# One transpose of the score maxima per batch in place of two, placed inside the key projections, with three other moves in the schedule

## The chip, the cores and the metric

The kernel runs on one core of one Trainium2 chip. The metric is the device time of one execution in microseconds (us); for the kernel before it is the median of three runs. The core has five queues that run beside each other and meet only at semaphores: TensorE (PE: matmuls, with its weight loads shown as PEld), VectorE (DVE), ScalarE (ACT), GpSimd (POOL) and SyncE (SP, which issues DMAs here).

## The reference

x is (32, 112, 512), the context (32, 375, 512); all is float32. Per batch: a layer norm of x, queries from it, keys and values from the 257 image rows and 118 text rows of the context with separate weights, an RMS norm on queries and keys, two softmax attentions over 16 heads of 32, their sum, an output projection and a residual:

```
q = rms_norm(linear(x, q_w, q_b), norm_q_w)
k = rms_norm(linear(ctx_txt, k_w, k_b), norm_k_w);  v = linear(ctx_txt, v_w, v_b)
k_img, v_img = the same from ctx_img with their own weights
out = attention(q, k, v) + attention(q, k_img, v_img)
x = x + linear(out, o_w, o_b)
```

Then a second layer norm, a router score for each row, the 14 best rows of each batch (`top_k`), and for these 448 rows alone a block of causal attention over all of them and a gated MLP, whose result is written back into the rows.

## The kernel before

The code has one hand-written instruction stream for each engine; there is no planner. What an engine does next is the order in which its stream lists the helpers, and each helper begins with the semaphore waits that it needs (`wait_ge`).

After a first stage (queries of all batches, weights), `over_batches` runs one pass for each of the 32 batches: pass 0 and pass 1, a hardware loop for passes 2 to 29, pass 30, and a pass 31 (`last`). In `body(i, n, m, p, q)`, i is the batch whose attention is made, n = i + 1 the one whose keys are projected, m = i + 2 the one whose context is loaded, p = i - 1 the one that gets its output projection, and q = i - 2 the one that gets its router score and rank. The passes follow each other without a barrier. After them comes the block on the chosen rows.

Matmuls of projections are made of three fp32r products (high by high, high by low, low by high), so each context tile is split on chip. ScalarE rounds it (`split_ctx`, L780, `ctx_hi`), and GpSimd subtracts the rounded part (L547, `ctx_lo`), once for the 118 text columns (part 0) and once for the 256 image columns (part 1). The semaphore `ctx_lo_done` counts these subtractions. `keys(n, k)` projects tile k of the keys with 12 matmuls of 512 columns (L1535 to L1537); tile 0 is text, tiles 1 and 2 are image. In front of tile 0 and of tile 1 it waits for the subtraction of its part (L1585).

For each of the four groups of four heads, `scores` (L1625) makes row scores in PSUM banks 2 to 5, `group_max` (VectorE, L1151 and L1152) takes a maximum for each head over text and over image keys into `top`. `turn_top` (TensorE, L1636) transposes `top`, once for groups 0 and 1 and once for groups 2 and 3, and ScalarE copies each result to `topT` (L834). `scores_T(i, g)` makes the scores once more, transposed, with the maxima subtracted: a small product of a 0/-1 matrix with `topT` for the text rows (L1660) and one for the image rows (L1664), and products of keys and queries in float32 (L1654). ScalarE takes the exponentials (L843, L845), GpSimd adds the two image tiles (`sum_image`, L581), VectorE adds one row (`add_tail`, L1157), and `weighted_values` (L1691) makes the four sums that `normalise` (VectorE, L1163 to L1169) divides. `o_hi` (ScalarE, L863) and `o_rest` (VectorE, L1173) split the result for `output` (TensorE, bank 1). `residual` (GpSimd, L589) adds the output bias to the reloaded x rows, `add_residual` and `ln2` (VectorE) and `normalise_h` (GpSimd) follow, then `score` (VectorE, L1200) and on GpSimd `output` (L585), which stands in the queue between the two parts of `split_ctx`. `turn_score` (TensorE, L1641) spreads the score of each row over a row of PSUM bank 7 and `ranks` (VectorE, L1191, L1193) counts how many are larger.

The order on TensorE around the change:

```
scores(i, 2); values(i, 1); turn_top(i, 0); scores(i, 3); keys(n, 0)
turn_top(i, 1); scores_T(i, 0); keys(n, 1); turn_score(q)
scores_T(i, 1); keys(n, 2); scores_T(i, 2)
```

Of the kernel before, what the change touches and what calls it, by code (L numbers as in the profile page):

```python
# [56 lines left out]
def build(nc, t, out):  # L57
    with ExitStack() as ctx:
# [109 lines left out]
        top = [p1(f"top{e}", [L, P]) for e in range(2)]  # L168
        topT = [p1(f"topT{e}", [P, L], F32R) for e in range(2)]
# [199 lines left out]
        def prob_of(g):  # L369
            return prob_txt_keys[g % 3], prob_img_keys[g % 3]  # L370

# [171 lines left out]
        def _(pool):  # L543
# [47 lines left out]
            def pre():  # L591
# [7 lines left out]
                nc.gpsimd.memset(top[0][:], 0.0)  # L599
                nc.gpsimd.memset(top[1][:], 0.0)  # L600
# [48 lines left out]
            def body(i, n, m, p, q):  # L649
# [33 lines left out]
            def last(i, p, q):  # L683
# [91 lines left out]
        def _(act):  # L775
# [56 lines left out]
            def turn_top(i, e):  # L832
                act.wait_ge(top_full, 2 * i + e + 1)
                nc.scalar.activation(topT[e][:], ps[:, 6, e * L:(e + 1) * L], ACT.Copy).then_inc(topT_ready, 1)  # L834
# [82 lines left out]
            def body(i, n, m, p, q):  # L917
# [42 lines left out]
            def last(i, p, q):  # L960
# [5 lines left out]
                turn_top(i, 0)  # L966
                token_squares(0)
                value_image(i, 1)
                token_squares(1)
                turn_top(i, 1)  # L970
                exps(i, 0)
# [134 lines left out]
        def _(dve):  # L1106
# [39 lines left out]
            def group_max(i, g):  # L1146
                dve.wait_ge(s_full, 4 * i + g + 1)
                if g % 2 == 0:
                    dve.wait_ge(top_full, 2 * i - 1 + g // 2 if not isinstance(i, int) or i else 0)
                rows = top[g // 2][:].rearrange("l (j r) -> l j r", j=GH)  # L1150
# [9 lines left out]
            def normalise(i, g):  # L1160
                dve.wait_ge(pv_full, 4 * i + g + 1)
                bank = ps[:, 6 + g % 2, 0:4 * L].rearrange("p (k q) -> p k q", k=4)
                nc.vector.reciprocal(rec[:], bank[:, 2:4]).then_inc(norm_step, 1)  # L1163
# [5 lines left out]
                nc.vector.scalar_tensor_tensor(oT[:, g], o_two[:, 0], v_bias[:, g:g + 1], o_two[:, 1], ALU.add, ALU.add).then_inc(pv_done, 1)  # L1169

# [16 lines left out]
            def ranks(q):  # L1187

                dve.wait_ge(score_turned, q + 1)
                score_row = ps[0:L, 7, 2 * L:3 * L]  # L1190
# [96 lines left out]
            def body(i, n, m, p, q):  # L1287
# [34 lines left out]
                add_tail(i, 2)  # L1322
                tail_keys(n)
# [18 lines left out]
            def last(i, p, q):  # L1342
# [8 lines left out]
                ranks(q)  # L1351
# [23 lines left out]
            ranks(B - 2)  # L1375
# [11 lines left out]
            ranks(B - 1)  # L1387
# [144 lines left out]
        def _(pe):  # L1532
# [95 lines left out]
            def turn_top(i, e):  # L1628
                pe.wait_ge(s_done, 4 * i + 2 * e + 2)
                if e:  # L1630
                    pe.wait_ge(topT_ready, 2 * i + 1)
# [109 lines left out]
            def body(i, n, m, p, q):  # L1741
# [30 lines left out]
                if q is not None:  # L1772
                    pe.wait_ge(rank_done, q + 1)
# [301 lines left out]
```

## Time and profile before

| what | value |
|---|---|
| three runs | 1526.75, 1527.26, 1528.58 us |
| profiled execution, its own time | 1524.64 us |
| its span | 1522.9 us |
| TensorE matmul busy | 1497.2 us (98%) |
| VectorE, ScalarE, GpSimd busy | 1182.6, 715.8, 688.5 us (78%, 47%, 45%) |
| chain that ended last | PE 89%, DVE 5%, ACT 3% |
| granted TensorE clock | 0.999 of full speed |

"Busy" is the share of time in which at least one instruction of the engine is under way. The chain that ended last is followed back from the last instruction of the span, at each step to what released it, so its shares tell which engine set the time. The passes over the batches lie between about 120 and 1172 us of the span. In the timeline views a row is one instruction or several merged ones, and "x4" is their number; matmuls are pipelined, so the time that one costs is the distance from start to start, not its duration.

### The profile page before, as it was taken

The numbers are of one execution on the slowest core, as the hardware profiler recorded it, in microseconds if no ns is written. First come the engines' busy times: TensorE is split into PE (matmuls) and PEld (weight loads), VectorE is DVE, ScalarE is ACT, GpSimd is POOL, SyncE is SP. The second block draws the span as 40 slices with busy tenths as digits, with TensorE's granted clock in tenths as the row PEclk, the third lists the DMA queues.
The fourth block names the chain that finished last, engine by engine and source line by source line (L and its number), as shares of the span: only waits on it lengthen the run. The fifth ranks groups of instructions, "written<-read, shape, count | busy, mean of one in ns | idle before, by whom it ended". The sixth has DMA issues, their size and how long they took to land.

```text
span 1522.9 us, 41381 instructions
## 1 busy us (share of the span) xinstructions
PE 1497.2 (98%) x16220; PEld 1186.7 (78%) x16220; DVE 1182.6 (78%) x1884; ACT 715.8 (47%) x1458; POOL 688.5 (45%) x727
## 2 busy tenths in 40 slices
PE   8999999999999999999999999999999999999997
PEld 6777777777777777777777777777777787778997
DVE  6765788888888888888888888888887686554986
ACT  5874444444444444444444444444445124655431
POOL 3543344454444454444444444544445692114752
PEclk9999999999999999999999999999999999999999
DMA  8961121211111221112221112121125524010000
GB/s 262 346 207 60 39 63 52 77 56 50 56 54 59 67 66 50 56 50 62 62 70 50 56 50 62 58 75 50 56 87 154 196 111 167 28 56 29 1 1 25
DMA packets 70199, 121.04 MB, mean 79 GB/s; under 512 B 21840, under 2 KB 36528, under 8 KB 68608
## 3 DMA queue, kind: packets, MB, share of 16 engines
q1 hardware_dynamic: 69312, 117.54, 23.9%
q0 software_dynamic: 832, 2.75, 0.7%
q8 instruction: 36, 0.59, 0.2%
q14 instruction: 19, 0.16, 0.0%
HBM read 89.93 MB, written 30.34 MB: 79 GB/s over the span
## 4 chain that ended last, share of the span: by engine, by line
PE 89%; DVE 5%; ACT 3%; issue 1%; DMA 1%; POOL 1%; ACTq 0%; DVEq 0%; POOLq 0%
PE ps L1535 21%; PE ps L1536 19%; PE ps L1537 18%; PE ps L1691 10%; PE ps L1654 6%; PE ps L1625 3%; PE ps L1596 3%; PE ps L1660 2%; PE ps L1900 2%; PE ps L1917 2%; PE ps L1909 1%; PE ps L1664 1%; DMA q_dram<-q_turned 1%; DVE rec L1163 1%; PE ps L1636 0%
## 5 line engine op out<-in xcount | busy, mean ns | idle before, releaser
L547 POOL TENSOR_TENSOR ctx_lo<-ctx_raw,ctx_hi 128x472 fp32r<-128x472 f32 (+1 forms) x62 | 112.8, 1819 | 192.8 <-ACT ctx_hi L780 192.8
L1163 DVE RECIPROCAL rec<-ps 128x224 f32<-128x224 f32 x128 | 198.3, 1549 | 1.1 <-PE ps L1691 0.9
L581 POOL TENSOR_TENSOR prob_img<-prob 128x448 f32<-128x448 f32 x93 | 107.9, 1160 | 149.3 <-ACT prob L845 149.3
L1152 DVE TENSOR_REDUCE top<-ps 112x4 f32<-112x1028 f32 x128 | 156.2, 1220 | 0.0
L1151 DVE TENSOR_REDUCE top<-ps 112x4 f32<-112x472 f32 x128 | 83.1, 649 | 72.9 <-PE ps L1625 72.9
L1654 PE MATMUL ps<-q_all,k_all 32*128 32x112 f32 (+1 forms) x3072 | 125.2, 274 | 0.0
L1535 PE MATMUL ps<-w_v_img_hi,ctx_hi 128*128 128x512 f32 x256 | 107.4, 419 | 0.0
L1535 PE MATMUL ps<-w_k_img_hi,ctx_hi 128*128 128x512 f32 x256 | 107.1, 418 | 0.0
L843 ACT ACTIVATE prob<-ps 119x448 f32<-119x448 f32 x96 | 52.4, 546 | 114.8 <-PE ps L1654 114.8
L1654 PEld LDWEIGHTS ps<-q_all,k_all 32*128 32x128 f32 (+1 forms) x3072 | 105.4, 184 | 0.0
L1536 PE MATMUL ps<-w_k_img_lo,ctx_hi 128*128 128x512 f32 x256 | 101.1, 395 | 0.0
L1536 PE MATMUL ps<-w_v_img_lo,ctx_hi 128*128 128x512 f32 x256 | 101.0, 395 | 0.0
L1537 PE MATMUL ps<-w_k_img_hi,ctx_lo 128*128 128x512 f32 x256 | 100.8, 394 | 0.0
L1537 PE MATMUL ps<-w_v_img_hi,ctx_lo 128*128 128x512 f32 x256 | 100.7, 393 | 0.0
L845 ACT ACTIVATE prob<-ps 128x896 f32<-128x896 f32 x96 | 87.7, 913 | 0.0
L780 ACT ACTIVATE ctx_hi<-ctx_raw 128x472 fp32r<-128x472 f32 x64 | 52.9, 827 | 69.8 <-PE ps L1537 69.8
L1137 DVE SCALAR_TENSOR_TENSOR proj<-proj,rstd,w_img 128x512 f32<-128x512 f32 x64 | 48.0, 750 | 45.4 <-POOL rstd L574 45.4
L1537 PE MATMUL ps<-hT_hi,ring_lo 128*128 128x448 f32 x224 | 81.9, 366 | 0.0
L813 ACT ACTIVATE sq_junk<-proj 128x513 bf16<-128x513 f32 (+1 forms) x96 | 61.1, 636 | 34.8 <-DVE proj L1131 34.8
L574 POOL TENSOR_TENSOR rstd<-sq_sum,neg_half 128x1 f32<-128x1 f32 x96 | 64.8, 675 | 16.0 <-ACT sq_junk L813 16.0
L1173 DVE SCALAR_TENSOR_TENSOR oT_lo<-o_space,oT_hi 128x448 fp32r<-128x448 f32 x31 | 39.7, 1282 | 40.7 <-ACT oT_hi L863 40.7
L1157 DVE SCALAR_TENSOR_TENSOR prob_img<-prob,ones_last,prob_img 23x448 f32<-23x448 f32 x93 | 64.5, 693 | 6.1 <-POOL prob_img L581 3.1
(358 smaller groups left out, 4410.7 us busy)
## 6 DMA issues: line engine op xcount, KB each, us to landing
ctx_raw<-in_ctx_dram SPq DMA_DIRECT2D x32, 748.0 KB, 4.2
xh_dram<-xh SPq DMA_DIRECT2D x32, 448.0 KB
xc<-in_xT_dram SPq DMA_DIRECT2D x28, 256.0 KB, 4.5
q_dram<-q_turned SPq DMA_DIRECT2D x28, 256.0 KB, 4.6
q_all<-q_dram SPq DMA_DIRECT2D x32, 224.0 KB, 3.1
out_dram<-out_sb SPq DMA_DIRECT2D x32, 224.0 KB, 2.3
xh<-in_x_dram SPq DMA_DIRECT2D x31, 224.0 KB, 2.9
proj<-in_x_dram SPq DMA_DIRECT2D x21, 256.0 KB, 5.1
```

What stands on the lines that cost most here:

```text
L547: nc.gpsimd.tensor_tensor(ctx_lo[:, :, cols], ctx_raw[:, :, cols], ctx_hi[:, :, cols].bitcast(F32), ALU.subtract).then_inc(ctx_lo_done, 1)
L574: nc.gpsimd.tensor_tensor(rstd1[:, k:k + 1], sq_sum[:, k:k + 1], neg_half[:], ALU.pow).then_inc(rms_inv, 1)
L581: nc.gpsimd.tensor_tensor(prob_img[:, g % 2], image[:, 0, :], image[:, 1, :], ALU.add).then_inc(img_summed, 1)
L845: nc.scalar.activation(image.rearrange("p c (j q) -> p j c q", j=GH), ps[:, 2:6, L:3 * L].rearrange("p j (c q) -> p j c q", c=2), ACT.Exp) ...
L1151: nc.vector.tensor_reduce(rows[:, :, 2 * g], ps[0:L, 2:6, 0:TXT], AX.X, ALU.max)
L1152: nc.vector.tensor_reduce(rows[:, :, 2 * g + 1], ps[0:L, 2:6, TAIL:CTX], AX.X, ALU.max).then_inc(s_done, 1)
L1163: nc.vector.reciprocal(rec[:], bank[:, 2:4]).then_inc(norm_step, 1)
L1535: nc.tensor.matmul(o_, a_hi, b_hi, start=start, stop=False)
L1536: nc.tensor.matmul(o_, a_hi, b_lo, start=False, stop=False)
L1537: return nc.tensor.matmul(o_, a_lo, b_hi, start=False, stop=stop)
L1654: made = nc.tensor.matmul(ps[0:rows, 2 + j, c * L:(c + 1) * L], k_all[head, g, at:at + rows], q_all[head, g, :], start=False, stop=stop)
L1691: last = nc.tensor.matmul(ps[HD * j:HD * (j + 1), bank, slot * L:(slot + 1) * L], left[0:rows, cols], right[0:rows, L * j:L * (j + 1)], st ...
```

## The change

`top` and `topT` become one tile each, and `turn_top` runs once per pass, for all groups; ScalarE copies once. In the passes its place on TensorE is behind `keys(n, 0)`, and the first six of the twelve matmuls of `keys(n, 1)` are put between it and `scores_T(i, 0)`. The other six and the first three of `keys(n, 2)` come between `scores_T(i, 0)` and `scores_T(i, 1)`, and the last nine between `scores_T(i, 1)` and `scores_T(i, 2)`. Inside `scores_T` the two products with `topT` now come first, before the products of keys and queries. `turn_score` writes to bank 2 and stands in front of the transposes of the new keys; `ranks` moves on VectorE to behind `add_tail(i, 2)`, and TensorE waits for it at the end of the pass. On GpSimd `residual` comes before the first `sum_image`; on ScalarE `o_hi` comes before the first exponentials; on VectorE the bias of key tile 1 is added before `add_tail(i, 0)`. A filler tile keeps the addresses of the other tiles. The last pass gets the same in its own order.

```diff
@@ gpsimd, body
                 split_ctx(n, 1)
-                sum_image(i, 0)
-                inverse_rms(n, 1)
                 if p is None:
                     pool.wait_ge(out_rows_loaded, 16 * 2)
                 else:
                     residual(p)
+                sum_image(i, 0)
+                inverse_rms(n, 1)
                 sum_image(i, 1)
@@ gpsimd, last
                 output(q)
+                residual(p)
                 pool.wait_ge(oT_lo_done, i)
+                pool.wait_ge(topT_ready, i + 1)
                 value_weights_lo(0, 0)
+                normalise_h(p)
                 value_weights_lo(0, 1).then_inc(w_lo_done, 1)
-                residual(p)
-                normalise_h(p)
@@ scalar, body
-                turn_top(i, 0)
-                turn_top(i, 1)
-                exps(i, 0)
+                turn_top(i)
                 if p is not None:
                     o_hi(p)
+                exps(i, 0)
@@ vector, body
                     o_rest(p)
+                add_bias(n, 2)
                 add_tail(i, 0)
-                if q is not None:
-                    ranks(q)
                 scale_k(n, 1)
-                add_bias(n, 2)
...
                 add_tail(i, 2)
+                if q is not None:
+                    ranks(q, ps[0:L, 2, 0:L])
                 tail_keys(n)
@@ tensor, keys
-            def keys(n, k):
+            def keys(n, k, chunks=range(KC)):
...
-                if k < 2:
-                    pe.wait_ge(ctx_lo_done, 2 * n + k + 1)
-                if not isinstance(n, int) or n or k == 2:
-                    pe.wait_ge(done, slot)
-                project(bank[0:rows], ctx_hi, ctx_lo, cols, w).then_inc(full, 1)
+                if 0 in chunks:
+                    if k < 2:
+                        pe.wait_ge(ctx_lo_done, 2 * n + k + 1)
+                    if not isinstance(n, int) or n or k == 2:
+                        pe.wait_ge(done, slot)
+                last = project(bank[0:rows], ctx_hi, ctx_lo, cols, w, chunks)
+                if KC - 1 in chunks:
+                    last.then_inc(full, 1)
@@ tensor, scores_T
-                    nc.tensor.matmul(ps[0:CHUNK_C, 2 + j, 0:L], pick_c[head, g, :], topT[g // 2][head, :], start=True, stop=False)
-                products(0, True)
+                    nc.tensor.matmul(ps[0:CHUNK_C, 2 + j, 0:L], pick_c[head, g, :], topT[head, :], start=True, stop=False)
                 for j in range(GH):
                     head = slice(HD * j, HD * (j + 1))
                     nc.tensor.matmul(..., pick_img[head, g, :],
-                                     topT[g // 2][head, :]..., start=True, stop=False)
+                                     topT[head, :]..., start=False, stop=False)
+                products(0, False)
                 products(1, False)
@@ tensor, body
                 values(i, 1)
-                turn_top(i, 0)
                 scores(i, 3)
                 keys(n, 0)
-                turn_top(i, 1)
+                turn_top(i)
+                keys(n, 1, range(0, 2))
                 scores_T(i, 0)
-                keys(n, 1)
-                if q is not None:
-                    pe.wait_ge(pv_done, 4 * i)
-                    turn_score(q)
+                keys(n, 1, range(2, KC))
+                keys(n, 2, range(0, 1))
...
                 scores_T(i, 1)
-                keys(n, 2)
+                keys(n, 2, range(1, KC))
...
                 scores_T(i, 2)
                 weighted_values(i, 0, n)
-                if q is not None:
-                    pe.wait_ge(rank_done, q + 1)
                 weighted_values(i, 1, n)
                 scores_T(i, 3)
                 if p is not None:
                     output(p)
                 pe.wait_ge(exp_done, 8 * i + 8)
+                if q is not None:
+                    turn_score(q, ps[0:L, 2, 0:L])
                 for k in range(1, 4):
                     turn(n, k)
                 values(n, 0, range(2 if p is None else 0, KC))
+                if q is not None:
+                    pe.wait_ge(rank_done, q + 1)
@@ tensor, last
                 output(p, range(0, 2))
                 scores(i, 3)
                 values(i, 1, range(3, 4))
-                output(p, range(2, 4))
-                turn_top(i, 1)
+                output(p, range(2, 3))
+                turn_top(i)
+                output(p, range(3, 4))
+                pe.wait_ge(pv_done, 4 * i)
+                turn_score(q, late_score_row)
                 scores_T(i, 0)
```

## Rows read from the trace of the kernel before

**Rows 1.** Windows view, one pass: window, then busy us (instructions) of each engine, clock, DMA.
```profile
602.38:635.16 32.78, 32.78 (x436) 25.65 (x435) 27.04 (x42) 15.04 (x30) 14.95 (x16) 1.00 0.19 58
```

**Rows 2.** Timeline of TensorE, one pass: start us, duration us, engine, line, operation, count.
```profile
618.77 0.43 PE L1625 MATMUL ps<-k_hi,q_hi 32*112 32x376 f32 x4
...
628.54 0.39 PE L1537 MATMUL ps<-w_k_hi,ctx_lo 128*118 128x512 f32 x1
...
628.78 0.26 PE L1636 MATMUL ps<-ident,top 112*128 112x112 f32 x1
...
628.97 0.32 PE L1660 MATMUL ps<-topT,pick_c 32*119 32x112 f32 x4
...
629.12 0.42 PE L1654 MATMUL ps<-q_all,k_all 32*119 32x112 f32 x8
...
629.30 0.35 PE L1664 MATMUL ps<-topT,pick_img 32*128 32x224 f32 x4
...
629.49 0.61 PE L1654 MATMUL ps<-q_all,k_all 32*128 32x112 f32 x16
...
630.02 0.50 PE L1535 MATMUL ps<-w_k_img_hi,ctx_hi 128*128 128x512 f32 x1
...
630.36 0.40 PE L1536 MATMUL ps<-w_k_img_lo,ctx_hi 128*128 128x512 f32 x1
...
633.10 0.32 PE L1660 MATMUL ps<-topT,pick_c 32*119 32x112 f32 x4
...
636.82 0.39 PE L1537 MATMUL ps<-w_k_img_hi,ctx_lo 128*128 128x512 f32 x1
...
637.14 0.32 PE L1660 MATMUL ps<-topT,pick_c 32*119 32x112 f32 x4
```

**Rows 3.** Timeline of GpSimd, same pass; in brackets the idle time before and its releaser.
```profile
625.68 1.30 POOL L585 TENSOR_TENSOR out_sb<-xh 112x512 f32<-112x512 f32 x1 [1.09 <-DVE out_sb L1200]
...
626.93 2.42 POOL L547 TENSOR_TENSOR ctx_lo<-ctx_raw,ctx_hi 128x1024 fp32r<-128x1024 f32 x1
...
631.69 1.16 POOL L581 TENSOR_TENSOR prob_img<-prob 128x448 f32<-128x448 f32 x1 [2.34 <-ACT prob L845]
...
633.71 1.49 POOL L589 TENSOR_TENSOR xh<-xh,out_bias 112x512 f32<-112x512 f32 x1
...
635.74 1.16 POOL L581 TENSOR_TENSOR prob_img<-prob 128x448 f32<-128x448 f32 x1 [0.54 <-ACT prob L845]
...
637.18 0.56 POOL L574 TENSOR_TENSOR rstd<-sq_sum,neg_half 128x1 f32<-128x1 f32 x1 [0.28 <-ACT sq_junk L813]
```

**Rows 4.** Timeline of ScalarE, same pass: the rounding of the image columns.
```profile
625.54 1.06 ACT L780 ACTIVATE ctx_hi<-ctx_raw 128x1024 fp32r<-128x1024 f32 x1 [2.25 <-PE ps L1537]
```

**Rows 5.** Timeline of the SP queue, same pass: two DMA issues.
```profile
627.75 0.34 SPq L481 DMA_DIRECT2D xh<-in_x_dram  x1
...
629.51 0.38 SPq L409 DMA_DIRECT2D ctx_raw<-in_ctx_dram  x1
```

**Rows 6.** Page, DMA issues: KB each, median us from issue to landing.
```profile
xh<-in_x_dram SPq DMA_DIRECT2D x31, 224.0 KB, 2.9
```

**Rows 7.** Timeline of VectorE, same pass.
```profile
626.59 1.22 DVE L1152 TENSOR_REDUCE top<-ps 112x4 f32<-112x1028 f32 x1
...
632.02 1.31 DVE L1173 SCALAR_TENSOR_TENSOR oT_lo<-o_space,oT_hi 128x448 fp32r<-128x448 f32 x1 [1.36 <-ACT oT_hi L863]
...
634.08 0.33 DVE L1191 SCALAR_TENSOR_TENSOR equal<-ps,score_now,later 112x112 f32<-112x112 f32 x1
...
634.81 0.93 DVE L1137 SCALAR_TENSOR_TENSOR proj<-proj,rstd,w_txt 118x512 f32<-118x512 f32 x1
...
637.77 0.75 DVE L1137 SCALAR_TENSOR_TENSOR proj<-proj,rstd,w_img 128x512 f32<-128x512 f32 x1 [1.43 <-POOL rstd L574]
...
649.32 0.65 DVE L1151 TENSOR_REDUCE top<-ps 112x4 f32<-112x472 f32 x1 [0.77 <-PE ps L1625]
```

**Rows 8.** Timeline of VectorE in the last pass: the same remainder with GpSimd idle.
```profile
1147.14 0.61 DVE L1173 SCALAR_TENSOR_TENSOR oT_lo<-o_space,oT_hi 128x448 fp32r<-128x448 f32 x1
```

More of the change, by code:

```diff
@@ L167, in build @@
         ones_all = p1("ones_all", [P, HD])
-        top = [p1(f"top{e}", [L, P]) for e in range(2)]
-        topT = [p1(f"topT{e}", [P, L], F32R) for e in range(2)]
+        top = p1("top", [L, P])
+        topT = p1("topT", [P, L], F32R)
+        p1("top_gap", [P, P + L])
         prob_img = p1("prob_img", [P, 2, GH * L])
@@ L830, in split_kq, with turn_top @@
                 copy_keys(n, 3).then_inc(kq_done, 1)
-            def turn_top(i, e):
-                act.wait_ge(top_full, 2 * i + e + 1)
-                nc.scalar.activation(topT[e][:], ps[:, 6, e * L:(e + 1) * L], ACT.Copy).then_inc(topT_ready, 1)
+            def turn_top(i):
+                act.wait_ge(top_full, i + 1)
+                nc.scalar.activation(topT[:], ps[:, 6, 0:L], ACT.Copy).then_inc(topT_ready, 1)
             def exps(i, g):
@@ L1147, in group_max @@
                 dve.wait_ge(s_full, 4 * i + g + 1)
-                if g % 2 == 0:
-                    dve.wait_ge(top_full, 2 * i - 1 + g // 2 if not isinstance(i, int) or i else 0)
-                rows = top[g // 2][:].rearrange("l (j r) -> l j r", j=GH)
+                if g == 0 and (not isinstance(i, int) or i):
+                    dve.wait_ge(top_full, i)
+                rows = top[:].rearrange("l (j r) -> l j r", j=GH)
                 nc.vector.tensor_reduce(rows[:, :, 2 * g], ps[0:L, 2:6, 0:TXT], AX.X, ALU.max)
@@ L1185, in ln2, with ranks @@
                 nc.vector.bn_aggr(ln2_mv[:], ln2_stats[:]).then_inc(ln2_step, 1)
-            def ranks(q):
+            def ranks(q, score_row):
                 dve.wait_ge(score_turned, q + 1)
-                score_row = ps[0:L, 7, 2 * L:3 * L]
                 nc.vector.scalar_tensor_tensor(equal, score_row, score_now[:], later[:], ALU.is_equal, ALU.mult).then_inc(rank_step, 1)
@@ L1350, in last @@
                 ln2(p)
-                ranks(q)
+                ranks(q, late_score_row)
                 normalise(i, 0)
@@ L1374, in _ @@
             hT_rest(3)
-            ranks(B - 2)
+            ranks(B - 2, late_score_row)
             def add_value_bias(m):
@@ L1386, in _ @@
             add_value_bias(0)
-            ranks(B - 1)
+            ranks(B - 1, late_score_row)
             choose(slice(EARLY_B, B), 2)
@@ L1635, in turn_top, with turn_score @@
                     pe.wait_ge(pro_done, 2)
-                nc.tensor.transpose(ps[:, 6, e * L:(e + 1) * L], top[e][:], ident[0:L, 0:L]).then_inc(top_full, 1)
-            def turn_score(p):
+                nc.tensor.transpose(ps[:, 6, 0:L], top[:], ident[0:L, 0:L]).then_inc(top_full, 1)
+            def turn_score(p, score_row):
                 pe.wait_ge(score_ready, p + 1)
-                nc.tensor.transpose(ps[0:L, 7, 2 * L:3 * L], score_now[:].to_broadcast([L, L]), ident[0:L, 0:L]).then_inc(score_turned, 1)
+                nc.tensor.transpose(score_row, score_now[:].to_broadcast([L, L]), ident[0:L, 0:L]).then_inc(score_turned, 1)
             def scores_T(i, g):
@@ L1664, in scores_T @@
                     nc.tensor.matmul(ps[:, 2 + j, L:3 * L].rearrange("p (c q) -> p c q", c=2), pick_img[head, g, :],
-                                     topT[g // 2][head, :].unsqueeze(1).to_broadcast([HD, 2, L]), start=True, stop=False)
+                                     topT[head, :].unsqueeze(1).to_broadcast([HD, 2, L]), start=False, stop=False)
+                products(0, False)
                 products(1, False)
@@ L1811, in last @@
                 values(i, 1, range(3, 4))
[L1812 to L1813 removed]
+                output(p, range(2, 3))
+                turn_top(i)
+                output(p, range(3, 4))
+                pe.wait_ge(pv_done, 4 * i)
+                turn_score(q, late_score_row)
                 scores_T(i, 0)
[L1815 to L1816 removed]
                 pe.wait_ge(b0_done, value_slot(i, 1)[3] + 1)
@@ L1835, in last @@
                 pe.wait_ge(pv_done, 4 * i + 4)
-                turn_score(p)
+                turn_score(p, late_score_row)
                 output_part(i, 3)
@@ L1858, in _ @@
             value_tile(2, range(0, 1))
-            turn_score(B - 1)
+            turn_score(B - 1, late_score_row)
             value_tile(2, range(1, 3))
```

34 lines of the change are left out of this document (16 added, 18 removed).

## The prediction, made before the changed kernel was run

> **What bounds the kernel now.** I read the views in the order page, windows, timelines. The page's chain that ended last lies 89% on TensorE, so only what lengthens or shortens TensorE's queue moves the time. The windows view of one pass shows TensorE busy for 32.78 of 32.78 us at full clock (1.00, the level of 2.4 GHz), with VectorE at 27.04 and the others at half or less [rows 1]. So a pass has no gap that an edit could close: a saving must be fewer or cheaper matmuls, and any wait that begins to hold TensorE is paid in full. The timelines then serve to find, for each moved instruction, who is only just in time.
>
> **The transposes.** Two projection matmuls follow each other every 0.23 us. Where the heads' scores follow a projection directly, L1660 starts 0.32 after the last wide matmul (636.82 to 637.14); with a transpose in between it is 0.43 (628.54 to 628.97) [rows 2]. A transpose there costs 0.10, and one of the two goes: -0.10 per pass. The other moves between two projections. The next weights are loaded under it, and a wide matmul whose weights were not loaded ahead has its successor 0.34 later (630.02 to 630.36) [rows 2], so I take 0.12 for it where it was 0.10: +0.02, bounds 0 and +0.04. `turn_score` is the same kind of transpose in either place: 0, bounds -0.02 and +0.02. The number of changes between wide matmuls and the 32-row matmuls of the heads stays the same, since the cut of `keys(n, 1)` and `keys(n, 2)` only shifts where they stand.
>
> **The new order in `scores_T`.** Before, the steps go topT text, text products, topT image, image products: 628.97, 629.12, 629.30, 629.49, and 0.53 from there to the next wide matmul [rows 2]. The first half, four steps of four matmuls, takes 0.52, the second half, also four steps, 0.53 with the change to full width in it. Nothing is dropped, and no row shows the new order. From above I bound it by 0. From below: if all steps went at the pace of the second half without its way out (0.53 less the 0.09 that such a change costs, 0.32 - 0.23), so 0.44, it would save 0.08 in each of four groups, 0.32 per pass. I take 0, because the steps that look long (0.15 and 0.19) and the short one between follow each other at a mean of 0.13, near to 0.11, and every load of weights is still there.
>
> **The wait that comes forward.** This is the term that decides. `keys(n, 1)` waits for `ctx_lo_done`, the subtraction of the image columns on GpSimd. That instruction runs from 626.93 for 2.42, to 629.35 [rows 3]. In the kernel before, TensorE has the transpose at 628.78 and then `scores_T(i, 0)`, and the projection starts at 630.02: 0.67 to spare. Now six of its matmuls come before `scores_T(i, 0)`, directly behind the transpose, and the wait stands in front of the first of them, although that one reads only `ctx_hi`. The queue is in order, and behind the wait stand `scores_T(i, 0)` and all the rest.
>
> Can the subtraction come earlier? It starts when GpSimd has done `output(q)` (625.68, 1.30), which VectorE's score released [rows 3]; its input from ScalarE is ready at 625.54 + 1.06 = 626.60 [rows 4]. None of these is moved, and they hang on VectorE's work since `scores(i, 1)` at 618.77, not on the transpose that is gone. So 629.35 stays. That it is the true end is seen on SP, which waits for the same count and then issues the next context load at 629.51 [rows 5].
>
> Step by step: the turn starts at 628.78 - 0.10 = 628.68. Without a wait the second matmul of the projection would start 0.12 + 0.23 later, at 629.03. With it the first weights are loaded at 629.35 plus the way of the semaphore, between 0.04 and 0.16 (SP's issue came 0.16 after, with an instruction in between); I take 0.10. Then 0.34 to the second matmul: 629.79. The stall is 0.76, bounds 0.70 and 0.82.
>
> The Trainium skill ("TensorE: Matmul & The Clock Gate", the steps of a matmul) says that TensorE pulls weight loads ahead of running matmuls, while the matmuls stay in program order. By the first half one might hope for the load to be done under the wait, which would make the stall 0.65; by the second, `scores_T` cannot slip past. I hold the load back too, since the wait stands before it in the stream.
>
> **The copy.** The turn's result must be on ScalarE and back before `scores_T(i, 0)`. It gets 6 x 0.23 = 1.39 even without the stall, more than the duration of turn and copy together. `group_max(i, 3)` ends at 626.59 + 1.22 = 627.81 [rows 7], 0.87 before the turn. Cost 0.
>
> **The residual on GpSimd.** After the subtraction it is idle for 2.34, to 631.69, where `sum_image` begins [rows 3], and now, with `scores_T(i, 0)` behind six matmuls, for 1.4 more. The x rows are loaded from 627.75 [rows 5] and land 2.9 later [rows 6], at 630.65; the 1.49 of `residual` end at 632.14. Its cover is that gap, cost 0; if the load came 1.5 later it would push the sum, the root and the scaling of the keys.
>
> The residual now falls beside `o_rest` on VectorE, at about 630.6. That one took 1.31 beside `sum_image` and 0.61 with GpSimd idle [rows 7, 8]. The Trainium skill ("SBUF — State Buffer", two separate sides) says that VectorE with two SBUF inputs and GpSimd lock each other out of a shared port pair, whoever is first holding it for its whole instruction; these rows agree. By that rule one of the two loses up to 0.7 or 1.3 there, and neither has anything urgent behind it: the next item, the bias of key tile 1, is waited for by nobody on TensorE until the exponentials of group 1 are made.
>
> **VectorE at the end of the pass.** `ranks` costs 0.73 (634.08 to 634.81) [rows 7] and moves to where VectorE has only 0.77 of idle before the next `group_max` at 649.32 [rows 7]. Count from `scores_T(i, 1)` at 633.10. TensorE now reaches the next `scores(i, 1)` (618.77 + 32.78 = 651.55) after 18.45 less three wide matmuls (0.69), plus the score's transpose (0.10): 17.86. VectorE's chain: `sum_image(i, 1)` ends at 635.74 + 1.16, the root behind it takes 0.56 [rows 3] and, now without its 0.28 of idle, ends at +4.36; `scale_k(n, 2)` began at 637.77 and all from there to the end of `group_max(i, 0)` (649.32 + 0.65 + 1.22 = 651.19 at the latest) is 13.42, less 0.77 idle, plus 0.73: +17.74. So 0.12 is left, or a little more where the two maxima overlap. No stall, but little cover; if it is gone, every further 0.1 costs 3 us in all.
>
> **The sum.** Per pass 0.76 - 0.10 + 0.02 = +0.68; passes 2 to 30 are 29: +19.7. In passes 0 and 1 there is no `output(q)`; the subtraction can start at 626.64 and ends at 629.06, stall 0.47, net 0.39 each: +0.8. The last pass has nothing of this wait; a transpose less, and other order on GpSimd: -0.1, bounds -1 and +1. Together +20.4. The profiled execution took 1524.64 (span 1522.9 and 1.7 around it): 1545.0. The median of the runs is 2.6 above it, so I give 1547.7.
>
> **Rivals.**
> 1. The new order in `scores_T` does save its bound: 0.32 in 31 passes, -9.9, so 1538. For it: the uneven steps; against: the same loads. A chance of 0.12, most of it for part of the amount.
> 2. VectorE becomes late for the next `scores(i, 1)`: a lockout such as that of `o_rest` (0.7) on its chain, less the 0.12, gives 0.58 for 29 passes, +17: 1565. For it the thin cover; against, the operations on that chain in its later part run while GpSimd is mostly idle. 0.07, mostly for a small part.
> 3. Not slower: the wait for `ctx_lo_done` does not bind, because GpSimd's spans are rough and the count is raised before the row's end. It decides at 628.68: released by then, the pass gains 0.08 and the time is 1527.3 - 2.5 = 1524.8; each 0.1 later costs 3 us. For it is only the warning on such spans, against it SP's issue at 629.51 and the fixed 2.42. 0.05.
> 4. The change does not do what it says, in that `scores_T(i, 0)` still waits for the copy. The stall would then show at L1660 and the copy would have to take over 1.39 where its kind is far shorter; with it 1550 or more. 0.01.
>
> The forecast itself has 0.75, its own range 1544 to 1551 (29 x 0.06 either way on the semaphore's way, the other small bounds, run to run). The range for 8 in 10, with parts of rivals 1 and 2, is 1539 to 1555. A measurement of this kernel tells 0.2%, 3 us, from no change. Slower 0.94 (forecast, rivals 1, 2, 4 and most in between), same 0.04, faster 0.02 (rival 3).
>
> **What would show it.** In the profile after, passes of 33.4 to 33.5 us, TensorE's matmuls with a gap before the first L1535 behind L1636, ended by GpSimd's L547, in every pass; L547 still 10.6 us behind `scores(i, 1)`; no gap before L1660 and none before L1625. Passes of 32.7 would prove me wrong at the wait; the first L1660 to the next wide matmul in 0.97 in place of 1.05 would be rival 1; a gap before the second L1625, ended by L1152, rival 2.

## The result, and the profile after

The changed kernel took 1551.59 us (median of 4 runs, 1551.52 to 1553.66) beside 1527.01 for the kernel before (4 runs, 1525.61 to 1528.58): ratio 1.0164, interval 1.015 to 1.0177. It is slower by 24.6 us, where 20.4 had been forecast. Its profiled execution has a span of 1549.8. One later run of the kernel before, made beside the experiments, was a slow one (1840.77 us at a granted clock of 0.743) and is left out of all ratios.

The windows view of one pass (us; busy us and instructions of TensorE, its weight loads, VectorE, ScalarE, GpSimd; clock, DMA share, GB/s) answers to [rows 1]:

```profile
628.30:661.80 33.50, 32.95 (x435) 25.40 (x434) 27.35 (x42) 14.86 (x28) 14.34 (x15) 1.00 0.18 57
```

A pass is 33.5 us long and TensorE is idle in 0.55 of it, at full clock (1.00). The waits view of TensorE (who waited for whom: us in total, times, longest) names the idle time. Its top row did not exist before; the next one did:

```profile
PE ps L1544 <- POOL ctx_lo L550: 16.4, 31, 0.6
PE ps L1637 <- ACT k_all L825: 3.7, 2, 2.4
```

The timeline of TensorE around the turn, in the same pass (start, duration, line; idle time before and its releaser in brackets), answers to [rows 2]:

```profile
641.00 0.26 PE L1646 MATMUL ps<-ident,top 112*128 112x112 f32 x1
641.80 0.19 PEld L1544 LDWEIGHTS ps<-w_k_img_hi,ctx_hi 128*128 128x128 f32 x1 [0.89 <-issue]
641.80 0.50 PE L1544 MATMUL ps<-w_k_img_hi,ctx_hi 128*128 128x512 f32 x1 [0.55 <-POOL ctx_lo L550]
642.14 0.40 PE L1545 MATMUL ps<-w_k_img_lo,ctx_hi 128*128 128x512 f32 x1
...
643.07 0.39 PE L1546 MATMUL ps<-w_k_img_hi,ctx_lo 128*128 128x512 f32 x1
643.38 0.32 PE L1670 MATMUL ps<-topT,pick_c 32*119 32x112 f32 x4
...
644.44 0.50 PE L1544 MATMUL ps<-w_k_img_hi,ctx_hi 128*128 128x512 f32 x1
...
664.31 0.38 PE L1701 MATMUL ps<-prob_img,ones_all 128*32 128x112 f32 x8
664.61 0.43 PE L1637 MATMUL ps<-k_hi,q_hi 32*112 32x376 f32 x4
```

GpSimd in the same pass, to be set beside [rows 3]:

```profile
638.01 1.29 POOL L588 TENSOR_TENSOR out_sb<-xh 112x512 f32<-112x512 f32 x1 [1.09 <-DVE out_sb L1209]
639.26 2.41 POOL L550 TENSOR_TENSOR ctx_lo<-ctx_raw,ctx_hi 128x1024 fp32r<-128x1024 f32 x1
642.89 1.28 POOL L592 TENSOR_TENSOR xh<-xh,out_bias 112x512 f32<-112x512 f32 x1 [1.22 <-DMA xh<-in_x_dram]
```

And VectorE, whose `o_rest` (L1183) and next maxima were steps of the prediction ([rows 7, 8]):

```profile
642.94 1.71 DVE L1183 SCALAR_TENSOR_TENSOR oT_lo<-o_space,oT_hi 128x448 fp32r<-128x448 f32 x1
...
663.17 1.22 DVE L1153 TENSOR_REDUCE top<-ps 112x4 f32<-112x1028 f32 x1
```

The subtraction `ctx_lo` ends at 639.26 + 2.41 = 641.67, the turn ran at 641.00, and the first wide matmul starts 0.13 after the subtraction's end. From turn to first wide matmul it is 0.80. The load of its weights (PEld) starts at 641.80 too, behind the wait. After that nothing is late: `scores_T(i, 0)` follows the six matmuls without a gap, and the maxima of the next group 0 end at 664.39, 0.22 before the scores that need them.

Where the 26.9 us between the two spans are: counting from the first `scores(i, 0)` to that of the last pass, 31 passes take 1042.1 us where they took 1019.8, so +22.4 (22.37 before rounding); the stage before them +1.8 in this execution; the last pass, up to the first matmul of the block on the chosen rows, +1.2; the wide matmuls of the gated MLP at the end +1.9; the rest of that block -0.3.

### The profile page after: what moved, and what is told of

Its sections match the earlier page's. It is cut to its first block, busy times and chain, and to the rows that moved or that the text cites. A ratio compares the mean times of both kernels' runs of the same rounds, so it can differ in the third digit from the quotient of the medians.

```text
span 1549.8 us, 41101 instructions
## 1 busy us (share of the span) xinstructions
PE 1504.9 (97%) x16188; PEld 1178.4 (76%) x16188; DVE 1166.6 (75%) x1884; ACT 710.5 (46%) x1426; POOL 678.7 (44%) x726
## 4 chain that ended last, share of the span: by engine, by line
PE 50%; issue 22%; POOL 14%; DVE 6%; ACT 5%; DMA 2%; POOLq 1%; SPq 0%; ACTq 0%; DVEq 0%
PE ps L1544 11%; PE ps L1546 9%; PE ps L1545 9%; POOL ctx_lo L550 7%; PE ps L1664 5%; PE ps L1701 5%; POOL prob_img L584 2%; PE ps L1670 2%; POOL out_sb L588 2%; PE ps L1909 2%; PE ps L1926 2%; DMA q_dram<-q_turned 2%; ACT prob L848 2%; POOL ln_rstd L567 1%; PE ps L1673 1%
## 5 line engine op out<-in xcount | busy, mean ns | idle before, releaser
L1544 PE MATMUL ps<-w_k_img_hi,ctx_hi 128*128 128x512 f32 x256 | 110.6, 432 | 16.4 <-POOL ctx_lo L550 16.4
L1664 PE MATMUL ps<-q_all,k_all 32*128 32x112 f32 (+1 forms) x3072 | 104.4, 266 | 0.0
L1132 DVE TENSOR_TENSOR proj<-ps,ki_bias 128x512 f32<-128x512 f32 x64 | 44.3, 692 | 77.5 <-PE ps L1546 76.5
L1664 PEld LDWEIGHTS ps<-q_all,k_all 32*128 32x128 f32 (+1 forms) x3072 | 94.9, 184 | 0.0
L1544 PEld LDWEIGHTS ps<-w_k_img_hi,ctx_hi 128*128 128x128 f32 x256 | 48.1, 188 | 40.9 <-issue 25.0
L816 ACT ACTIVATE sq_junk<-proj 128x513 bf16<-128x513 f32 (+1 forms) x96 | 61.1, 636 | 24.6 <-DVE proj L1132 24.6
```

The source lines that it names most:

```text
L1544: nc.tensor.matmul(o_, a_hi, b_hi, start=start, stop=False)
L1664: made = nc.tensor.matmul(ps[0:rows, 2 + j, c * L:(c + 1) * L], k_all[head, g, at:at + rows], q_all[head, g, :], start=False, stop=stop)
```

## The experiments

Twelve more programs ran, one of them the changed kernel again without an edit. Each ratio is to the kernel before, run beside it on the same chip; its median was between 1527.01 and 1528.73, so times of two rows can differ by 1 to 2 us for that alone. "Pass" is the mean of passes 5 to 27, from one `scores(i, 0)` to the next.

| kernel | time us | ratio, interval | pass us |
|---|---|---|---|
| before | 1527.01 | 1 | 32.780 |
| after | 1551.59 | 1.0164 [1.0150, 1.0177] | 33.508 |
| after, again | 1549.93 | 1.0148 [1.0133, 1.0164] | 33.527 |
| high products first | 1526.75 | 0.9996 [0.9987, 1.0004] | 32.727 |
| turn inside tile 0 | 1524.80 | 0.9982 [0.9973, 0.9991] | 32.683 |
| the same, old product order | 1525.34 | 0.9984 [0.9975, 0.9992] | 32.675 |
| after, old product order | 1548.37 | 1.0136 [1.0121, 1.0151] | 33.479 |
| no cover for the copy | 1540.71 | 1.0088 [1.0073, 1.0103] | 33.187 |
| subtraction ahead of output | 1594.88 | 1.0455 [1.0433, 1.0477] | 34.998 |
| before, projection forward | 1661.41 | 1.0881 [1.0866, 1.0897] | 37.228 |
| the same with two supports | 1550.36 | 1.0141 [1.0123, 1.0158] | 33.476 |
| after, `o_hi` back | 1556.29 | 1.0174 [1.0157, 1.0191] | 33.645 |
| after, residual back | 1552.56 | 1.0155 [1.0138, 1.0172] | 33.510 |
| after, bias back | 1550.75 | 1.0148 [1.0131, 1.0165] | 33.510 |

The theory was that of the prediction: the wait for `ctx_lo_done`, now ahead of `scores_T(i, 0)`, is the whole loss. The rivals were the order inside `scores_T`, the copy, VectorE at the end of the pass, and that the other moves matter.

**High products first.** The six matmuls ahead of `scores_T(i, 0)` are those that read only `ctx_hi`; the wait for `ctx_lo` stands behind it.

```diff
-                keys(n, 1, range(0, 2))
+                keys_high(n)      # waits for ctx_hi_done; 6 products of chunks 0 to 2
                 scores_T(i, 0)
-                keys(n, 1, range(2, KC))
+                keys_low(n)       # waits for ctx_lo_done; the other 6
```

> The changed kernel with everything kept but this: the six matmuls between the turn and the first transposed scores are now the six of key tile 1 that read only the rounded context (two for each of three chunks); the products with the remainder come behind those scores, and the wait for the remainder with them. Same matmuls, same number before and behind. My theory (the wait for GpSimd's remainder, moved forward, costs 0.79 us in each pass and is nearly the whole loss): passes of 32.70 to 32.74 us in place of 33.51, no gap before the first wide matmul behind the turn, about 1525 us in all, 2 us under the kernel before. Rival (the moved residual, ranks and bias addition, or the new order of products, cost the time and the gap would only move elsewhere): passes stay above 33.2, time above 1541.

It was as expected: the wait's row is gone from the view of waits, and the pass is 0.78 shorter than in the changed kernel. TensorE's timeline, with the load of weights (PEld) that now starts together with the turn:

```profile
630.01 0.26 PE L1664 MATMUL ps<-ident,top 112*128 112x112 f32 x1
630.01 0.19 PEld L1610 LDWEIGHTS ps<-w_k_img_hi,ctx_hi 128*128 128x128 f32 x1
630.03 0.48 PE L1610 MATMUL ps<-w_k_img_hi,ctx_hi 128*128 128x512 f32 x1
630.35 0.40 PE L1611 MATMUL ps<-w_k_img_lo,ctx_hi 128*128 128x512 f32 x1
```

Nothing else of the change was touched, the same products stand behind the turn, and the subtraction takes as long. So the wait costs 0.78 per pass, and the rest of the change gains 0.05. This is shown, not only argued.

**Turn inside tile 0.** The other way out of the wait: the turn moves into `keys(n, 0)`, whose last three matmuls cover the copy, and tile 1 stays whole behind `scores_T(i, 0)`.

```diff
-                keys(n, 0)
+                keys(n, 0, range(0, 3))
                 turn_top(i)
-                keys(n, 1, range(0, 2))
+                keys(n, 0, range(3, KC))
                 scores_T(i, 0)
-                keys(n, 1, range(2, KC))
+                keys(n, 1)
```

> The changed kernel with the turn moved forward by three matmuls, into the projection of key tile 0, whose last chunk (three matmuls, 0.69 us) now covers the copy; key tile 1 is whole behind the first transposed scores, as in the kernel before. My theory: the maxima are ready 0.2 us before the turn, turn to copied maxima takes about 0.6 us, so no wait anywhere; the projection of tile 1 starts 0.4 us after the remainder is ready. Passes of 32.70 us, about 1525 us. Rival (the copy, not the remainder, holds TensorE): a gap before the first product with the copied maxima and passes above 33.

With its twin of the old product order (below) it is the fastest kernel here, 0.18% below before, with an interval that leaves out 1. Its windows view shows TensorE without a gap, and its pass is 0.097 shorter than before's, about the 0.10 of the one transpose that is gone:

```profile
617.50:650.16 32.66, 32.66 (x435) 25.40 (x434) 26.24 (x42) 14.75 (x28) 14.77 (x15) 1.00 0.19 59
```

Over 31 passes that is 3.0 us, near the 2.5 by which the medians differ. In its profiled execution 1.5 of it are lost in pass 1 (34.16 for 32.69), which runs partly at 1.2 GHz; the last section shows it.

**After, again,** without an edit, and **the old product order** in the changed kernel and in the fastest one:

```diff
+                products(0, True)         # between the two products with topT, as before
                 ...
-                                     ..., start=False, stop=False)
-                products(0, False)
+                                     ..., start=True, stop=False)
```

> The changed kernel itself once more, beside the others on one chip. In its first trace the last 130 us (the gated MLP, which the change does not touch) took 2 us longer than in every other trace. If that belongs to the program: again 1551.5 and 136 us from the last attention product to the last matmul. If it was that chip or that run: 134 us, and 1549.5.

> The changed kernel with the order of products inside the transposed scores put back (text maxima, text products, image maxima, image products). My theory, from the trace of after where both orders take 1.057 us a group: no difference, passes of 33.51, 1551.6 us within 1. Rival (the new order gains up to 0.08 us a group, hidden behind another loss): about 10 us slower, passes of 33.8.

> The version with the turn inside the projection of key tile 0, and inside the transposed scores the order of the kernel before. From the traces so far the old order is 0.03 us a pass shorter (33.48 against 33.51 with the stall in both). If that is a property of the order: passes of 32.65 and about 1 us less than with the new order, near 1524. If the 0.03 came from the stall, passes of 32.68.

In the two pairs the passes with the new order are longer, by 0.01 with no stall (32.683 for 32.675) and by 0.03 to 0.05 (33.508 and 33.527 for 33.479). That can't be put down to the order: counted from the starts in the timelines, the mean distance of two wide matmuls that follow each other in passes 5 to 27 lies between 231.6 and 232.5 ns in the fourteen profiles, in kernels of either order, and over the 84 of a pass that makes 0.08. Rival 1, 0.32 per pass saved, is out. The changed kernel with the old order was 3.2 us faster than expected (1548.37 for 1551.6): 0.9 of it are the passes, and 1.9 a pace of the block at the end that changes from program to program (last section). The changed kernel run again has the longer pace of that block once more, as expected for a property of the program, though its time was nearer to the other value, 1549.5.

**No cover for the copy.** Tile 1 whole behind `scores_T(i, 0)`, nothing between the turn and the products that need its copy.

```diff
                 turn_top(i)
-                keys(n, 1, range(0, 2))
                 scores_T(i, 0)
-                keys(n, 1, range(2, KC))
+                keys(n, 1)
```

> The changed kernel with key tile 1 whole behind the first transposed scores: one turn, and nothing between it and the first use of the copied maxima. My theory: no wait for the remainder, but one for the copy, 0.3 from the turn to ScalarE, 0.26 copy, 0.05 back, against 0.19 before: a stall of 0.42, passes of 33.10, about 1537. It tells what the half projection was put there to hide: half of what it cost. Rival (the copy hides itself): passes of 32.7.

The wait for the copy, paid in full, is cheaper than the wait for the subtraction, though dearer than expected (passes of 33.19 for 33.10). TensorE, then ScalarE:

```profile
637.06 0.26 PE L1646 MATMUL ps<-ident,top 112*128 112x112 f32 x1
637.76 0.32 PE L1670 MATMUL ps<-topT,pick_c 32*119 32x112 f32 x4 [0.44 <-ACT topT L837]
```
```profile
637.36 0.26 ACT L837 ACTIVATE topT<-ps 128x112 fp32r<-128x112 f32 x1 [1.88 <-PE ps L1646]
```

From turn to product it is 0.70 where it was 0.19 [rows 2], so the cover is worth 0.51; less the transpose saved that is +0.41 per pass, as measured. The change bought a cover for 0.51 with a wait of 0.79.

**Subtraction ahead of output.** The stall attacked from GpSimd's side: `split_ctx(n, 1)` before `output(q)`.

```diff
                 split_ctx(n, 0)
+                split_ctx(n, 1)
                 if q is not None:
                     output(q)
-                split_ctx(n, 1)
```

> The changed kernel with one exchange on GpSimd: the remainder of the image columns is made ahead of the sum for the output (1.30 us), not behind it. My theory: the remainder is then ready 0.29 us earlier (ScalarE's rounding is the next to hold it), so the stall falls from 0.79 to 0.50 and passes go from 33.51 to 33.22, in all 8 us less than the changed kernel, 1543. The x rows are loaded 2.4 us later and the residual and first image sum with them, which should be absorbed. Rival (the stall is not set by the remainder): passes stay at 33.5. Second rival (the late residual reaches TensorE): passes above 33.5.

This missed by 52 us. The stall at the wait did shrink (turn to first wide matmul 0.57 in place of 0.80), but two new rows are above it in the view of waits:

```profile
PE ps L1701 <- DVE prob_img L1158: 24.2, 19, 2.1
PE ps L1637 <- DVE top L1153: 11.1, 26, 0.5
PE ps L1544 <- POOL ctx_lo L550: 9.5, 31, 0.3
```

GpSimd's timeline of a pass says why:

```profile
1013.68 1.29 POOL L588 TENSOR_TENSOR out_sb<-xh 112x512 f32<-112x512 f32 x1
1018.84 1.27 POOL L592 TENSOR_TENSOR xh<-xh,out_bias 112x512 f32<-112x512 f32 x1 [3.88 <-DMA xh<-in_x_dram]
1020.07 1.16 POOL L584 TENSOR_TENSOR prob_img<-prob 128x448 f32<-128x448 f32 x1
```

The x rows can be loaded only after `output(q)` has read the buffer. With that one later, the load lands later (`residual` starts 15.5 behind `scores(i, 1)`, where it was 11.8), and `residual`, which since the change stands ahead of the sums, holds the first sum. All of VectorE's pass follows it, down to the maxima that the next `scores(i, 1)` needs. That is the prediction's "if the load came 1.5 later it would push the sum, the root and the scaling", and the sign of its rival 2, a wait for the maxima at the second L1637, from this cause and not from a lockout.

**Before, projection forward.** The change's one costly move alone, in the kernel before, with both turns and everything else as they were.

```diff
                 turn_top(i, 1)
+                keys(n, 1, range(0, 2))
                 scores_T(i, 0)
-                keys(n, 1)
+                keys(n, 1, range(2, KC))
```

> The kernel before with one part of the change alone: the first six matmuls of key tile 1, and so the wait for its remainder, stand between the second turn and the first transposed scores. Two turns, ranks, residual and everything else as before. My theory: the wait alone makes the loss. The remainder is ready 0.57 us behind the second turn, stall about 0.68, passes of 33.46 to 33.52 (32.78 before), about 1548 us, with a gap ended by GpSimd in every pass. Rival (it needs the other moves too): passes below 33.0 and less than 1534 us.

The expectation failed by 113 us. The wait for `ctx_lo` is as expected; above it stands one for VectorE:

```profile
PE ps L1694 <- DVE prob_img L1157: 61.3, 29, 2.1
PE ps L1535 <- POOL ctx_lo L547: 13.2, 29, 0.5
```

Its timelines, ScalarE first, then VectorE:

```profile
619.32 0.55 ACT L843 ACTIVATE prob<-ps 119x448 f32<-119x448 f32 x1 [2.94 <-PE ps L1657]
...
620.56 0.57 ACT L863 ACTIVATE oT_hi<-o_space 128x448 fp32r<-128x448 f32 x1
...
626.61 0.64 ACT L813 ACTIVATE sq_junk<-proj 128x513 bf16<-128x513 f32 x1 [3.19 <-DVE proj L1131]
627.24 0.52 ACT L843 ACTIVATE third_txt<-ps 119x448 f32<-119x448 f32 x1
```
```profile
621.17 1.29 DVE L1173 SCALAR_TENSOR_TENSOR oT_lo<-o_space,oT_hi 128x448 fp32r<-128x448 f32 x1 [3.45 <-ACT oT_hi L863]
...
623.94 2.03 DVE L1137 SCALAR_TENSOR_TENSOR proj<-proj,rstd,w_txt 118x512 f32<-118x512 f32 x1
625.89 0.68 DVE L1131 TENSOR_TENSOR proj<-ps,ki_bias 128x512 f32<-128x512 f32 x1
628.00 0.76 DVE L1137 SCALAR_TENSOR_TENSOR proj<-proj,rstd,w_img 128x512 f32<-128x512 f32 x1 [1.43 <-POOL rstd L574]
628.79 1.55 DVE L1157 SCALAR_TENSOR_TENSOR prob_img<-prob,ones_last,prob_img 23x448 f32<-23x448 f32 x1
```

Read from the top: the exponentials come later by the six matmuls and the stall, `o_hi` stands behind them on ScalarE, and `o_rest`, first in VectorE's queue, waits 3.45 for it. Behind `o_rest` stand `add_tail(i, 0)`, the ranks, a scaling of 2.03 and only then the bias of key tile 1 (625.89). ScalarE idles 3.19 for that bias, and its squares, root and scaling (628.00) stand in front of `add_tail(i, 1)`, which `weighted_values(i, 1)` needs: a wait of 2.11 on TensorE. That wait costs more than itself; windows of TensorE after it (busy us and instructions, clock, DMA share, GB/s):

```profile
630.40:631.20 0.80, 0.80 (x24) 0.98 0.00 0
631.20:632.40 1.20, 1.20 (x25) 0.50 0.00 0
...
633.50:635.00 1.50, 1.50 (x5) 0.64 0.58 137
635.00:637.00 2.00, 2.00 (x14) 1.00 0.04 12
```

Some 3 us after it run at the lower level, 1.2 GHz: the 16 products of `scores_T(i, 3)` take 1.00 where they took 0.54, and the output projection of twelve matmuls 3.92 in place of 2.87. With 2.32 for the stalled block and the 0.68 of the first wait this makes 4.5 of the 4.6 us by which this pass is longer than [rows 1] (4.4 in the mean of the passes).

**The supports.** Two of the change's small moves added to that kernel: `o_hi` before the exponentials and the bias before `add_tail(i, 0)`.

```diff
@@ scalar, body
-                exps(i, 0)
                 if p is not None:
                     o_hi(p)
+                exps(i, 0)
@@ vector, body
                     o_rest(p)
+                add_bias(n, 2)
                 add_tail(i, 0)
                 if q is not None:
                     ranks(q)
                 scale_k(n, 1)
-                add_bias(n, 2)
```

> The kernel before with the six matmuls of keys(n, 1) forward, and with two more moves of the change: o_hi ahead of the first exponentials (ScalarE), and the bias of key tile 1 ahead of add_tail(i, 0) (VectorE). Theory read from the trace of the kernel with only the projection forward (1661, passes of 37.3): the damage there came from o_hi standing behind the late exponentials, so that o_rest, add_tail and with them the bias of tile 1 were late and squares(n, 2) held the exponentials of group 2 on ScalarE. With both moved o_rest can run from about 621 in that pass's time in place of 624 and the bias right behind it, so the passes fall to 33.4 to 33.7 and the time to 1545 to 1555. Rival: the place of residual and ranks (untouched here) matters as much; then passes stay at 35 or more and the time at 1590 or more.

It fell from 1661 to 1550, with passes of 33.48, so the reading of the timelines holds and the place of `residual` and `ranks` is not needed for it. VectorE now:

```profile
642.48 0.63 DVE L1173 SCALAR_TENSOR_TENSOR oT_lo<-o_space,oT_hi 128x448 fp32r<-128x448 f32 x1
645.56 0.69 DVE L1131 TENSOR_TENSOR proj<-ps,ki_bias 128x512 f32<-128x512 f32 x1 [2.46 <-PE ps L1537]
```

The bias waits for TensorE, not TensorE for it. Then each of three moves taken back alone from the changed kernel: `o_hi(p)` behind `exps(i, 0)`; `residual(p)` behind `sum_image(i, 0)` and `inverse_rms(n, 1)`; `add_bias(n, 2)` behind `add_tail(i, 0)` and `scale_k(n, 1)`.

> The changed kernel with only o_hi put back behind the first exponentials on ScalarE. Theory: o_hi waits about 1.4 us longer than before the change, o_rest (VectorE) follows it, and the bias of tile 1 with it; exponentials of group 2 are held by squares(n, 2): a wait of weighted_values(1) for the row sum comes back, passes of 34.5 to 37, time 1580 to 1650. Rival: the bias, which here stands directly behind o_rest and ahead of add_tail, is early enough, and residual early takes load from the end: passes of 33.5 to 33.6, 1550 to 1553.

> The changed kernel with only residual put back behind sum_image(i, 0) and the first root on GpSimd. Theory: residual (1.3 to 1.5 us) then stands between the first and the second image sum, where sum_image(i, 1) is due about 1.4 us after the root; it takes 0 to 0.5 us from a chain that has about 0.1 to 0.2 us to spare at the next group_max(i, 0): passes of 33.5 to 34.0, time 1550 to 1566. Rival: its place does not matter, 33.5 and 1549 to 1552; the other rival, it is one of the supports without which the projection can't come forward: 35 or more, 1590 or more.

> The changed kernel with only the bias of key tile 1 put back behind add_tail(i, 0) and scale_k(n, 1) on VectorE. Theory: the bias is then later by the 0.3 of add_tail and about 1 us of scale_k, and by add_tail's own wait for sum_image(0), together about 2 us; squares(n, 2) on ScalarE, which stands ahead of the exponentials of group 2, becomes late by up to that, but those exponentials come 1.4 us later than before the change too. Cost 0 to 0.6 per pass: 33.5 to 34.1, 1550 to 1569. Rival: it holds the exponentials as in the kernel with only the projection forward: 35 or more, 1590 or more.

`o_hi` back costs 0.14 per pass, far less than the theory gave it; its rival was near. The view of waits does not list that 0.14, but the timelines have it. TensorE, then VectorE:

```profile
635.73 0.37 PE L1701 MATMUL ps<-prob_img,ones_all 128*32 128x112 f32 x8
636.18 0.43 PE L1637 MATMUL ps<-k_hi,q_hi 32*112 32x376 f32 x4
```
```profile
634.91 1.22 DVE L1153 TENSOR_REDUCE top<-ps 112x4 f32<-112x1028 f32 x1
```

`scores(i, 1)` starts 0.45 behind the last block of the sums, where in the changed kernel it was 0.30 (664.31 to 664.61), and only 0.05 behind the end of the maxima that it needs (636.13), in each of passes 5 to 27. So VectorE holds TensorE there: this is the place of rival 2, and `o_rest` takes 1.29 or 1.30 again in this kernel. With the residual back the maxima end 0.07 to 0.09 ahead of `scores(i, 1)`, where it was 0.22: no time is lost, but most of the cover. The bias back costs nothing that can be told.

The kernel with the two supports shows that they together take away 3.8 us per pass. In the changed kernel either of the two is enough without the other. Whether one alone would be enough in the kernel before, where `ranks` and `residual` stand in their old places, was not run.

## Why the prediction was right, and where not

- **The wait.** Right in place and cause, and the first kernel above isolates it. The second wide matmul was put at 13.83 us behind `scores(i, 0)` (turn at 12.71 plus 1.11) and is there at 13.84, and the subtraction ends 10.6 behind `scores(i, 1)` as before. The stall was 0.79 for 0.76: the release took 0.13 (641.67 to 641.80) where I had 0.10 to the load of weights. A load finished under the wait would have given 0.65; it was not. The Trainium skill ("TensorE: Matmul & The Clock Gate", Part 2) says that weight loads are pulled ahead of matmuls in flight. The first experiment agrees: the load of the first wide matmul starts with the turn (630.01), the matmul 0.02 later. The changed kernel shows that a load does not pass a wait that stands in front of it in the queue (641.80, 0.80 behind the turn).
- **The transpose removed, -0.10.** Right where nothing waits: the kernel with the turn inside tile 0 gains 0.097. In the changed kernel it is worth nothing of itself: the subtraction's end is tied to VectorE's work since `scores(i, 1)`, so TensorE only reaches the wait earlier. The kernel with both turns, the same wait and the two supports has passes of 33.476, the changed kernel with the same old product order 33.479. My sum had this in it, since the stall was counted from 628.68 and not 628.78.
- **The product order, 0.** Right within 0.05, which is as much as can be told.
- **The copy, 0.** Right: no wait for it; uncovered it costs 0.51.
- **VectorE at the end of the pass.** 0.12 of slack was forecast, "or a little more", and 0.22 was there; 0.05 of that is the way from the maxima to the scores, as the kernel with `o_hi` back shows, so 0.17 could be lost. Rival 2 did not come, but it was near: with `o_hi` back VectorE holds the pass by 0.14, with `output(q)` delayed it holds it too.
- **The residual, 0.** Right in time. `o_rest` and the residual do fall together: in 22 passes the residual takes 1.55 to 1.75 and `o_rest` 0.62 or 0.63, in 7, the one shown among them, the residual takes 1.26 to 1.29 and `o_rest` 1.35 to 1.75. TensorE waited for neither.
- **`o_hi`, the early bias.** The step failed in its meaning, not in its number. I gave these moves no price, as work beside other work. Together they carry the projection's move: without both it costs 4.4 us a pass and not 0.7.
- **The size.** The 31 passes took 22.4 more and not 20.5 (29 of +0.68 and two of +0.39), which is 1.9 of the 4.2 us that the forecast's difference (20.4) was short. A pass of the loop was +0.73, pass 0 +0.64, pass 1 +0.39 and pass 30 +0.90.
- **Outside the passes.** The last pass was mis-sized: put at -0.1 with a bound of +1, it was +1.2. Two of its waits are 0.96 longer in sum: 0.29 at the one turn, for the last maxima (L1646 for `top`), where none was, and 0.84 for `o_space` where it was 0.17. The changed kernel again has 0.23 for the latter, and its last pass is +0.6; what decides between these is open. The MLP, in which nothing was changed, was +1.9 in both profiles of this program, and the stage before the passes +1.8 in this one. Against that the medians lie 24.6 apart and the profiled spans 26.9, because the profiled execution before was 2.4 below its median. My own range for the likeliest case, 1544 to 1551, was passed by 0.6 in the first timing and held in the second (1549.93). Outside the passes the spans differ by 4.6 us (1.8 + 1.2 + 1.9 - 0.3) that the sum did not foresee; the passes themselves, which it was about, it had within a tenth.

## What to carry to other kernels

In an in-order queue that is full, a wait moves with the instruction behind which you put it: before you bring half a projection forward as cover, compare the end of its latest input with its new place, and take the products whose inputs are ready. Ask what the cover is worth and what it costs; here it hid 0.51 and waited 0.79. And small moves on other engines that seem free may be what keeps a large one from costing six times its price (4.4 for 0.7 here), so take moves out singly and together before you call one idle.

## What the runs showed of the hardware

- A wait of 2.1 us in the middle of a pass was followed, 0.8 us later, by some 3 us at 1.2 GHz. The waits of 0.55 us in every pass of the changed kernel were not: the clock stayed at 1.00. And one and the same wait can go either way. In the kernel with only the projection forward 26 of its 29 waits of 2.1 us for `prob_img` were followed by the lower level, from 0.3 to 2.0 us behind their end, and three were not. One of the three (TensorE's busy us and instructions, clock, DMA share, GB/s):

```profile
480.30:482.42 2.12, 0.00 (x2) 1.00 0.00 0
482.42:486.00 3.58, 3.58 (x50) 1.00 0.10 22
```

At the start of pass 1 TensorE waits for the first keys in every kernel here, 2.14 to 2.39 us. In six of the fourteen profiles (waits of 2.28 to 2.38) the lower level followed, in eight (2.14 to 2.39) it did not. In the kernel with the turn inside tile 0:

```profile
155.80:158.15 2.35, 0.00 (x1) 1.00 0.00 0
158.15:159.20 1.05, 1.05 (x16) 0.51 0.00 0
159.20:160.20 1.00, 1.00 (x28) 0.50 0.00 0
```

and in the changed kernel:

```profile
157.20:159.56 2.36, 0.00 (x1) 1.00 0.00 0
159.56:160.50 0.94, 0.94 (x28) 1.00 0.00 0
```

What decides between the two is open.
- The gated MLP at the end, with the same 576 matmuls of 448 columns in all programs, runs at one of two paces, whatever the edit. Windows of 100 us inside it, of before and of the changed kernel (TensorE's busy us and matmuls first):

```profile
1410.00:1510.00 100.00, 99.76 (x492) 92.32 (x492) 89.20 (x90) 36.94 (x69) 57.55 (x43) 1.00 0.00 1
```
```profile
1435.00:1535.00 100.00, 99.63 (x482) 90.54 (x483) 88.03 (x88) 36.49 (x68) 57.43 (x43) 1.00 0.00 1
```

That is 203 ns a matmul in nine of the fourteen profiles, 207 in the other five (both of the changed kernel among them), at full clock in each. From the first of the 576 to the last it is 119.7 us in the nine and 121.6 in the five, so 1.9 us. What sets it is open.
- `o_rest` took 0.61 to 0.63 with GpSimd idle, mostly 1.29 to 1.31 beside a sum of 1.14 to 1.16, and beside the residual one of the two instructions was long and the other not: `o_rest` 1.35 to 1.75 with the residual at 1.26 to 1.29, or 0.62 to 0.63 with the residual at 1.55 to 1.75. The Trainium skill ("SBUF — State Buffer", two separate sides) has VectorE with two SBUF inputs and GpSimd exclude each other for a whole instruction; these rows agree.
